# Self-attention: query and key rows of heads 4 to 15 moved into their stacks by transfers

## The chip, the cores and the metric

One core of a Trainium2 chip runs the whole program. The time is the device time of one execution in microseconds, the median of three runs for the kernel before. Its engines are TensorE (PE, with its weight loads as PEld), VectorE (DVE), ScalarE (ACT), GpSimd (POOL) and SyncE (SP), which here only issues transfers.

## The reference, cut to what matters

Four sequences of 1024 tokens with 256 channels pass through four blocks: an expert block (its own stage of the program, not touched but for one order), and then two transformer blocks and a last cross-attention. All is float32. The first transformer block:

```python
t_sa, t_ca, t_mlp = jnp.split(jax.nn.silu(t_emb) @ tp_w + tp_b, 3, axis=-1)
h = layernorm(x, ln1_g, ln1_b)
h = mha(h, h, sa_wq, sa_bq, sa_wk, sa_bk, sa_wv, sa_bv, sa_wo, sa_bo)      # 16 heads of 16
x = x + h + t_sa[:, None, :]
h = layernorm(x, ln3_g, ln3_b)
h = mha(h, context_emb, ca_wq, ca_bq, ca_wk, ca_bk, ca_wv, ca_bv, ca_wo, ca_bo, mask=mask)   # 77 context rows
x = x + h + t_ca[:, None, :]
h = layernorm(x, ln2_g, ln2_b)
x = x + jax.nn.gelu(h @ w1 + b1, approximate=False) @ w2 + b2 + t_mlp[:, None, :]
# mha: softmax(q k^T / 4) v for each head
```

The second block is the same with modulated norms (weights `L2_...`, query, key and value in one matrix `qkv_w`); the third has one cross-attention. So there are 4 x 2 = 8 self-attentions, 12 cross-attentions and 8 MLPs in a run.

## The kernel before

The program is one Bass block for each engine. The four sequences pass one after the other through the loop `blocks`. The order of the work in one pass is the list `PASS`, which `pass_schedule` writes out; every engine walks that list and does its part of each step, and semaphores count the steps. The names are tuples: a module (`L1sa`, `L1ca`, `L1mlp`, `L2sa`, ...) and a step. `n` is a half of 512 tokens, `c` a half of the 256 channels, `g` a group of four heads.

In a self-attention the steps are: `N` normalise, `T` transpose, `P` project queries or keys (128 channels, 512 tokens), `V` values, `K` stacks, `A` products for the row maxima, `both` and `M` the maxima's minima and transpose, `S` scores, `PV` products with the values, `O`, `R`, `W`, `Q`, `OT`, `aT` the outputs, `o` output projection.

A product of float32 precision is made of a high part (`qh`, `kh`, float32r) and a residual (`ql`, `kl`) that GpSimd computes (L1937). The stacks `qs` and `ks` hold for each pair of heads, one at partitions 0 to 63 and one at 64 to 127, the rows of 16 channels three times (high, high or low, low), so that one product gives all three terms. Two more rows hold the negated row maxima in `qs` (`MAXROW`) against ones in `ks`, and a mask. A `K` step fills the stacks of its pairs with selection products on TensorE (`sel`, two for each pair), and a copy on ScalarE (`a`, `A`) or VectorE (`d`) with a bias that sets the row of ones. `A`, `a` differ in whether the product reads all 128 rows or the pair's own 32.

`A` (g, n, t, j) is a pair of products into two banks of PSUM; VectorE reduces 128 x 1024 numbers to two maxima (L1791). There are 4 x 2 x 4 x 4 = 128 of them, of which 20 stand before the first scores. After that the list has for each unit of four score products (`S`, one for each head of a group, exponential on ScalarE, L1470) three further `A` steps in the first four units, and two later, until all are done. A unit is (g, n, kt), 64 in all; the first eight are group 0, half 0, and the ninth begins group 0, half 1.

SyncE issues its transfers in an order of its own (`send_outputs`, which walks the same list). After each block of 128 tokens it sends the maxima of four heads into their rows of `qs` (`send_maxima`, L655, four transfers of 512 bytes), for the very first half from the transposed `mrow` (L669). `S` of unit (g, n, 0) waits until all of that group and half have landed (`maxima_stacked`). The MLP's weights come at the start of a pass (L636, L637) and, for the second block, behind the first MLP.

TensorE takes PSUM banks in a self-attention from `shared`: before the last of the first 16 maxima any of seven, later fixed ones; bank 7 sums `PV`.

## Time and profile before

| | us |
|---|---|
| three runs | 3683.58, 3699.18, 3698.08 |
| median | 3698.08 |
| profiled execution | 3701.89 |
| its span, first to last instruction | 3700.1 |
| TensorE busy in the span | 3394.4 (92%) |
| ScalarE busy | 2302.2 (62%) |
| VectorE busy | 2223.0 (60%) |
| GpSimd busy | 871.0 (24%) |

The passes of `blocks` begin at about 641, 1407, 2171 and 2934 us. A busy TensorE is not one at its peak, and the busy share is a mean over stages with different limits. It has to be read stage by stage: how full each engine is in a stretch, and which wait ends last there. The granted clock (PEclk) is 1.00 at 2.4 GHz and 0.50 at 1.2 GHz.

### The profile page before, as it was taken

What the parts mean: (1) busy time and instruction counts of PE and PEld (TensorE: products, weight loads), DVE (VectorE), ACT (ScalarE), POOL (GpSimd) and SP (SyncE); (2) the same over time, 40 slices, a digit from 0 to 9 for tenths busy, and PEclk for the clock granted to TensorE, in tenths of its full rate; (3) what the DMA queues carried; (4) which work ended last, traced back from release to release, by engine and by line L of the source; (5) the groups of instructions that cost most, each with busy time, mean ns of one, the idle gap of its engine ahead of it and who ended that gap; (6) DMA issues with size and microseconds to landing.
All of it is one profiled execution on the core that took longest, in us unless ns stands there. A gap on an engine that the chain in (4) does not pass through costs nothing.

```text
span 3700.1 us, 60840 instructions
## 1 busy us (share of the span) xinstructions
PE 3394.4 (92%) x22433; PEld 2000.9 (54%) x22433; DVE 2223.0 (60%) x3645; ACT 2302.2 (62%) x3983; POOL 871.0 (24%) x578
## 2 busy tenths in 40 slices
PE   8999998999899898998998889989998899899988
PEld 6767766444643564446444744455446444564465
DVE  2323324794397556953794559746955488549654
ACT  2333332787578555875786457865875578658764
POOL 0322322103400431015103420052024200340061
PEclk8989989999999999999999999999999999999999
DMA  5011012110100001110010010100100101000100
GB/s 184 1 36 35 2 36 63 32 16 26 39 8 14 13 13 57 14 30 31 13 16 15 12 57 11 22 26 26 14 19 13 58 7 26 24 28 11 22 13 13
DMA packets 226988, 101.25 MB, mean 27 GB/s; under 512 B 159951, under 2 KB 210322, under 8 KB 226582
## 3 DMA queue, kind: packets, MB, share of 16 engines
q1 hardware_dynamic: 201734, 77.21, 8.4%
q10 hardware_dynamic: 24976, 20.15, 1.8%
q8 instruction: 196, 3.21, 0.4%
q14 instruction: 82, 0.67, 0.1%
HBM read 79.31 MB, written 9.96 MB: 24 GB/s over the span
## 4 chain that ended last, share of the span: by engine, by line
PE 79%; DVE 12%; ACT 5%; issue 2%; POOL 1%; DMA 0%; SPq 0%; ACTq 0%; DVEq 0%; POOLq 0%
PE ps L736 76%; DVE mxh L1791 4%; PE ps L1184 2%; DVE ctxk L1740 2%; DVE ow L1823 1%; ACT probs L1470 1%; DVE tok L1526 1%; PE ps L1045 1%; DVE small L1510 1%; DVE x L1757 1%; DVE mx L1788 1%; POOL small L1847 1%; ACT qs L1439 1%; ACT whole L1424 1%; ACT hT L1256 1%
## 5 line engine op out<-in xcount | busy, mean ns | idle before, releaser
L1470 ACT ACTIVATE probs<-ps 128x512 f32<-128x512 f32 (+1 forms) x2176 | 1220.4, 639 | 222.3 <-PE ps L736 169.7
L1791 DVE TENSOR_REDUCE mxh<-ps 128x2 f32<-128x1024 f32 x1024 | 1232.1, 1220 | 101.2 <-PE ps L736 96.3
L736 PE MATMUL ps<-probs,v 128*32 128x256 f32 (+2 forms) x8064 | 732.8, 435 | 9.7 <-ACT probs L1470 6.3
L736 PE MATMUL ps<-ks,qs 64*128 64x512 f32 x2048 | 502.4, 491 | 51.5 <-DVE mxh L1791 23.3
L736 PEld LDWEIGHTS ps<-ks,qs 64*128 64x128 f32 x2048 | 193.0, 183 | 445.8 <-issue 347.7
L736 PE MATMUL ps<-qs,ks 64*128 64x512 f32 x2048 | 425.5, 413 | 4.0 <-DVE mxh L1791 3.0
L1911 POOL TENSOR_TENSOR hT<-hT,tok 128x512 f32<-128x512 f32 (+1 forms) x32 | 40.9, 1279 | 1221.1 <-DMA tok<-weights_of_outputs 1221.1
L736 PEld LDWEIGHTS ps<-probs,v 128*32 128x32 f32 (+1 forms) x8064 | 160.0, 107 | 302.7 <-ACT probs L1470 249.1
L736 PEld LDWEIGHTS ps<-qs,ks 64*128 64x128 f32 x2048 | 244.0, 184 | 127.6 <-ACT probs L1470 105.9
L1788 DVE TENSOR_REDUCE mx<-ps 128x4 f32<-128x312 f32 x384 | 166.3, 477 | 150.9 <-PE ps L736 147.4
L736 PE MATMUL ps<-hT,slot 128*128 128x512 f32 x448 | 235.5, 659 | 21.2 <-issue 8.5
L1439 ACT ACTIVATE qs<-ps,cols 128x512 fp32r<-128x512 f32 x288 | 180.4, 688 | 106.4 <-PE ps L736 106.0
L736 PE MATMUL ps<-slot,hT 128*128 128x256 f32 x896 | 217.6, 388 | 9.3 <-ACT hT L1485 9.3
L1847 POOL TENSOR_TENSOR small<-small 128x4 f32<-128x4 f32 x66 | 67.8, 1028 | 654.9 <-DVE small L1520 654.9
L1877 POOL TENSOR_TENSOR hidl<-hid,hidh 128x512 fp32r<-128x512 f32 x96 | 125.5, 1309 | 356.6 <-ACT hid L1348 356.4
L1757 DVE TENSOR_TENSOR x<-x,ps 128x512 f32<-128x512 f32 x80 | 54.9, 686 | 238.2 <-PE ps L736 238.2
L736 PEld LDWEIGHTS ps<-slot,hT 128*128 128x128 f32 x896 | 164.1, 190 | 60.0 <-issue 29.3
L1937 POOL TENSOR_TENSOR ql<-whole,qh 128x512 fp32r<-128x512 f32 x80 | 101.9, 1274 | 280.2 <-ACT whole L1424 280.2
L1345 ACT ACTIVATE hidh<-ps,cols 128x512 fp32r<-128x512 f32 x96 | 66.2, 689 | 162.6 <-PE ps L736 162.5
L1919 POOL TENSOR_TENSOR hidl<-hid,hidh 128x512 fp32r<-128x512 f32 x128 | 161.5, 1295 | 7.1 <-ACT hid L1494 5.8
L1045 PE MATMUL ps<-ident,tok 128*128 128x128 f32 x448 | 76.9, 310 | 80.4 <-DVE tok L1526 62.4
L736 PEld LDWEIGHTS ps<-kz,qs 128*128 128x128 f32 x768 | 123.1, 213 | 46.0 <-issue 17.6
(226 smaller groups left out, 5893.9 us busy)
## 6 DMA issues: line engine op xcount, KB each, us to landing
qs<-mx SPq DMA_DIRECT2D x896, 0.5 KB, 2.0
slot<-in_L_w SPq DMA_DIRECT2D x8, 1024.0 KB, 10.0
slot<-in_L_fc_w SPq DMA_DIRECT2D x8, 1024.0 KB, 5.2
hT<-ow SPq DMA_DIRECT2D x48, 128.0 KB, 2.7
tok<-weights_of_outputs SPq DMA_DIRECT2D x192, 32.0 KB, 1.9
xin<-in_x ACTq DMA_DIRECT2D x5, 1024.0 KB, 5.9
x_after_block<-x ACTq DMA_DIRECT2D x20, 256.0 KB, 2.3
xin<-x_after_block SPq DMA_DIRECT2D x5, 1024.0 KB, 5.5
```

The source lines that it names most:

```text
L736: return pe.matmul(out, lhsT, rhs, start=start, stop=stop)
L1045: ins = pe.transpose(ps[:, b, i * P:(i + 1) * P], tok[:, t, c * P:(c + 1) * P], ident[:])
L1184: ins = pe.transpose(ps[:, a, i * P:(i + 1) * P], ow[:, o:o + P], ident[:])
L1439: ins = act.activation(qs[:, pair, n * HALF:(n + 1) * HALF], ps[:, b, :], ACT.Identity, bias=qs_rows)
L1470: ins = act.activation(dst, src, ACT.Exp, scale=SCALE)
L1757: dve.tensor_tensor(xx, xx, src, ALU.add).then_inc(dve_done, M.add(dve_done, (tag, "x", t2)))
L1788: dve.tensor_reduce(mx[:, z, t, j0:j0 + GH], ps[:, a, 0:GH * SP_].rearrange("p (j s) -> p j s", s=SP_), AX.X, ALU.max, negate=True).then_i ...
L1791: dve.tensor_reduce(mxh[:, z, t, j // 2, j % 2, :], ps[:, a:a + 2, :], AX.X, ALU.max, negate=True).then_inc(dve_done, M.add(dve_done, name))
L1847: pool.tensor_tensor(rstd[:, tt], ve[:, tt], nhalf[:, tt], ALU.pow).then_inc(pool_done, M.add(pool_done, (tag, "rstd", h)))
L1877: pool.tensor_tensor(hidl0[:, (E * n + e) % 2, m % 4, :], hid0[:, m % 4, :], hidh0[:, (E * n + e) % 2, m % 4, :].bitcast(F32), ALU.subtrac ...
L1919: pool.tensor_tensor(hidl[:, n, m, :], hid[:, n, m, :], hidh[:, n, m, :].bitcast(F32), ALU.subtract).then_inc(pool_done, M.add(pool_done, ...
L1937: pool.tensor_tensor(lo[:, c, part], whole[:, whole_of(name)[0], 0:kn], hi[:, c, part].bitcast(F32), ALU.subtract).then_inc(pool_done, M.a ...
```

## The change

Selection products remain for heads 0 to 3 only (pairs 0 and 1 of channels 0 to 127). The rows of heads 4 to 15 are moved into their places in `qs` and `ks` by transfers from the projections' high and low parts. For this the columns of the query and key weights and biases are laid out on the host so that the heads of a group of rows lie a fixed step apart (`heads_apart`), and every second row of such a tile belongs to the same half of the pairs. Each transfer writes 16 partitions: `X` step part 1 moves two pairs (heads 4 to 7, 128 KB a transfer, into `group_moved`), part 2 four pairs (heads 8 to 15, 256 KB a transfer, into `heads_moved`). A part has twelve of these and two of ones into the maxima's row of `ks`. The stack's places are set anew (48 rows, then the maxima's and the mask's row), and the products read 48 or 49 rows instead of 64.

The projections' parts get places of their own: those of channels 0 to 127 in the exponentials' buffers 2 and 3, so the third unit's exponentials wait for part 1, and those of channels 128 to 255 in the MLP's weight slots 2 and 3. So the MLP's weights are now loaded behind part 2 of `X` in the same module, and SyncE waits there for `heads_moved`.

The lead-in has another order: 16 first maxima by key halves, projections of the other halves between them. TensorE may use all eight banks before the first scores. `A` waits for its own pair and half only. In a cross-attention `OT` stands behind the next products; in an MLP two `up` steps stand ahead of the second half's transposes, the second `rsqrt` is at its normalisation, and the split of the normalised rows goes channel half by channel half.

```diff
@@ -48,9 +48,11 @@
 FF = 4 * D
 FM = FF // P
 STACK = 64
-MAXROW = 32
-MASKROW = 33
+MAXROW = 48
+MASKROW = 49
+PLACES = {"q": ((0, 16), (32,)), "k": ((0, 32), (16,))}
 PAIRS = HEADS // 2
+PROBS_KEPT = 2
...
     def self_lead(tag):
 
         first = tag == "L1sa"
-        put(tag, ("T", 0), *[("load",)] * first, ("P", "q", 0, 0), ("P", "k", 0, 0), ("N", 1), ("T", 1), ("P", "q", 1, 0),
-            ("K", "dddd", "q", 0, 0), ("K", "aaaa", "k", 0, 0), ("P", "k", 0, 1), ("P", "q", 0, 1), ("V", 0), ("K", "ddaa", "k", 0, 1), *[("mask",)] * first)
+        put(tag, ("T", 0), *[("load",)] * first, ("P", "q", 0, 0), ("P", "k", 0, 0), ("N", 1), ("T", 1),
+            ("K", "dd--", "q", 0, 0), ("K", "aa--", "k", 0, 0), *[("mask",)] * first)
...
     def self_attention(tag, follow):
         maxima, last = [], []
+        moves = [("X", 2, which, e) for e in range(2) for which in "qk"]
         for g in range(GROUPS):
             for n in range(NH):
+                if (g, n) == (0, 0):
+                    maxima += [("A", g, n, t, j) for i in range(2) for t in range(TPH) for j in (i, 2 + i)]
+                    maxima += [("both", g, n, TPH - 1)]
+                    last = [("M", g, n)]
+                    continue
                 for t in range(TPH):
                     maxima += [("A", g, n, t, 0)] + last + [("A", g, n, t, j) for j in range(1, GH)]
-                    last = [("both", g, n, t)] if (g, n) != (0, 0) else []
-                if (g, n) == (0, 0):
-                    maxima += [("both", g, n, TPH - 1)]
-                    last = [("M", g, n)]
+                    last = [("both", g, n, t)]
+                    if g < 2:
+                        last += moves[:2]
+                        moves = moves[2:]
         maxima += last
 
-        def halves(which, c, n, who="a"):
-            return [("K", 2 * who + "--", which, c, n), ("K", "--" + 2 * who, which, c, n)]
-
-        beside = ([("P", "k", 1, 0)] + halves("q", 0, 1) + [("P", "q", 1, 1)] + halves("k", 1, 0) + [("P", "k", 1, 1)]
-                  + [w for k in halves("q", 1, 0, "A") + halves("q", 1, 1, "A") for w in (k, None)] + halves("k", 1, 1, "A"))
+        def pair_of(which, n):
+            return ("K", "aa--", which, 0, n)
+
+        beside = {2: [("P", "k", 0, 1)], 4: [("P", "q", 0, 1)], 6: [pair_of("k", 1)], 8: [pair_of("q", 1)],
+                  9: [("X", 1, which, e) for e in range(2) for which in "qk"] + [("V", 0)], 11: [("P", "q", 1, 0)], 13: [("P", "k", 1, 0)],
+                  15: [("P", "q", 1, 1)], 17: [("P", "k", 1, 1), ("add",)]}
...
-        first_slot = GH * TPH
-        for i in range(first_slot):
-            more(i + 1)
-            put(tag, *[w for w in beside[i:i + 1] if w])
-        more(first_slot + 1)
-        put(tag, *beside[first_slot:], ("add",))
-        lead = first_slot + 4
-        more(lead)
+        lead = GH * TPH + 4
+        for i in range(1, lead + 1):
+            more(i)
+            put(tag, *beside.get(i, []))
...
@@ -252,12 +257,12 @@
         for u in range(len(units) + lag):
             if u < len(units):
                 put(tag, ("S",) + units[u] + (0,), *last[4 * u:4 * u + 2])
-            if u > lag:
-                put(tag, ("OT",) + units[u - lag - 1][:2])
             if u >= lag:
                 put(tag, ("PV",) + units[u - lag], ("O",) + units[u - lag][:2])
             if u < len(units):
                 put(tag, ("S",) + units[u] + (2,), *last[4 * u + 2:4 * u + 4])
+            if u > lag:
+                put(tag, ("OT",) + units[u - lag - 1][:2])
...
-        put(follow, ("T", 0), ("N", 1), ("T", 1), *[("up", 0, m) for m in range(FM)])
+        put(follow, ("T", 0), ("N", 1), ("up", 0, 0), ("up", 0, 1), ("T", 1), *[("up", 0, m) for m in range(2, FM)])
...
-def stacks_for(tag, engine, g, n):
-
+def stacks_for(tag, engine, g, n, j):
+
+    cross = KIND[tag] == "cross"
+    pairs, halves = ((2 * g, 2 * g + 1), (0,)) if cross else ((2 * g + j // 2,), (j % 2,))
     return [(tag,) + stack for k in PASS if k[:2] == (tag, "K") for _, pair, stack, by in stack_pairs(*k[2:])
-            if by == engine and pair * 2 // GH == g and (k[3] == "k" or k[5] == n)]
+            if by == engine and pair in pairs and (k[5] in halves if k[3] == "k" else k[5] == n)]
...
+def heads_apart(a, blocks):
+
+    import numpy as np
+
+    columns = np.arange(a.shape[-1])
+    for block in range(blocks):
+        for first, heads in ((P // 2, GH), (P, 2 * GH)):
+            at = block * D + first
+            columns[at:at + heads * HD] = at + np.arange(heads * HD).reshape(heads, HD).T.ravel()
+    return a[..., columns]
...
+        kept = {(which, 0): [place(f"{which}0{part}", [P, N], F32R, offset=r2 + 4 * (PROBS_KEPT * GH * HALF + (2 * i + k) * N))
+                             for k, part in enumerate("hl")] for i, which in enumerate("qk")}
...
+        kept.update({(which, 1): [place(f"{which}1{part}", [P, N], F32R, offset=at[0] + 4 * (2 * 2048 + (2 * i + k) * N))
+                                  for k, part in enumerate("hl")] for i, which in enumerate("qk")})
...
+        def heads_of(tag, which, part, e):
+
+            c, first = (0, P // 2) if part == 1 else (1, 0)
+            dst, pairs = (qs, ks)[which == "k"], slice(PAIRS // KC // 2, PAIRS // KC) if part == 1 else slice(PAIRS // KC, PAIRS)
+            return [(dst[stacked(e, row, row + HD), pairs, :].bitcast(F32), tile[first + e:P:2, :].bitcast(F32))
+                    for tile, rows_at in zip(parts_of(tag, which, c), PLACES[which]) for row in rows_at]
...
-                sp.dma_start(W1, wide(T["L1_w1"])).then_inc(slot_loaded[2], M.add(slot_loaded[2], "L1mlp", LOADED))
-                sp.dma_start(W2, wide(T["L1_w2"])).then_inc(slot_loaded[3], M.add(slot_loaded[3], "L1mlp", LOADED))
...
+                def send_heads(tag, part, which, e):
+
+                    moved, c = group_moved if part == 1 else heads_moved, part - 1
+                    end = (tag, part) if (which, e) == ("k", 1) else None
+                    for n in range(NH):
+                        sp.wait_ge(pool_done, upto(pool_done, (tag, "P", which, c, n)))
+                    if which == "k":
+                        pairs = slice(PAIRS // KC // 2, PAIRS // KC) if part == 1 else slice(PAIRS // KC, PAIRS)
+                        sp.dma_start(ks[stacked(e, MAXROW, MAXROW + 1), pairs, :].bitcast(F32), ones[0:(pairs.stop - pairs.start) * N // 32, :]
+                                     ).then_inc(moved, M.add(moved, None, LOADED))
+                    for i, (dst, src) in enumerate(heads_of(tag, which, part, e)):
+                        sp.dma_start(dst, src).then_inc(moved, M.add(moved, end if i == 2 else None, LOADED))
+                    if part == 2 and end:
+                        sp.wait_ge(heads_moved, upto(heads_moved, end))
+                        for dst, s, name in (W1, 2, {"L1sa": "L1_w1", "L2sa": "L2_fc1_w"}[tag]), (W2, 3, {"L1sa": "L1_w2", "L2sa": "L2_fc2_w"}[tag]):
+                            then = tag[:2] + "mlp"
+                            sp.dma_start(dst, wide(T[name])).then_inc(slot_loaded[s], M.add(slot_loaded[s], then, LOADED))
...
-                    for _, kind, g, n, *rest in [k for k in PASS if k[0] == tag and k[1] in ("both", "M", "O", "R", "W")]:
+                    for _, kind, g, n, *rest in [k for k in PASS if k[0] == tag and k[1] in ("both", "M", "O", "R", "W", "X")]:
+                        if kind == "X":
+                            send_heads(tag, g, n, *rest)
+                            continue
...
-                sp.wait_ge(mm_done, upto(mm_done, ("L1mlp", "up", NH - 1, FM - 1)))
-                sp.dma_start(W1, wide(T["L2_fc1_w"])).then_inc(slot_loaded[2], M.add(slot_loaded[2], "L2mlp", LOADED))
-                sp.wait_ge(mm_done, upto(mm_done, ("L1mlp", "o", 3)))
-                sp.dma_start(W2, wide(T["L2_fc2_w"])).then_inc(slot_loaded[3], M.add(slot_loaded[3], "L2mlp", LOADED))
...
-            USED = [0] * 7
+            USED = [0] * 8
...
+                        if kind == "S":
+                            scored.add(tag)
+                        if tag in scored and asked[tag] < GROUPS * NH * TPH * GH:
                             among = (0, 2) if count == 2 else (4, 5, 6)
+                        elif tag in scored:
+                            among = range(8 - count)
                         else:
-                            count = 2 if kind == "A" else 1
-                            among = range(8 - count)
+                            among = range(9 - count)
...
-                        pe.wait_ge(act_done, upto(act_done, *stacks_for(tag, "act", g, n), *act_was))
-                        pe.wait_ge(dve_done, upto(dve_done, *stacks_for(tag, "dve", g, n), *dve_was))
+                        pe.wait_ge(act_done, upto(act_done, *stacks_for(tag, "act", g, n, j), *act_was))
+                        pe.wait_ge(dve_done, upto(dve_done, *stacks_for(tag, "dve", g, n, j), *dve_was))
...
+                            if g == 1:
+                                pe.wait_ge(group_moved, upto(group_moved, (tag, 1)))
+                            elif g > 1:
+                                pe.wait_ge(heads_moved, upto(heads_moved, (tag, 2)))
                             pair, i = 2 * g + j // 2, j % 2
                             for e in range(2):
-                                r = stacked(e, 0, STACK)
+                                r = stacked(e, 0, MAXROW)
...
                 for c in range(KC):
                     act.wait_ge(mm_done, upto(mm_done, (tag, "T", n, c)))
                     act.activation(hTh[:, c, half], ps[:, M.where((tag, "T", n, c)), :], ACT.Identity, bias=shift(c), scale=gain(c))
-                for c in range(KC):
+                    act.wait_ge(mm_done, upto(mm_done, (tag, "T", n, KC - 1)))
...
+                        if not cross and (u, j) == (PROBS_KEPT, 0):
+                            act.wait_ge(group_moved, upto(group_moved, (tag, 1)))
...
-                    elif kind == "o" and step[1] % 2 and tag in NEXT_LN:
+                    elif kind == "o" and step[1] % 2 and tag in NEXT_LN and not (step[1] == 3 and NEXT_LN[tag] in ("ln2", "ln6")):
                         rsqrt(upto, NEXT_LN[tag], step[1] // 2)
+                    elif kind == "N" and step[1] and KIND[tag] == "mlp":
+                        rsqrt(upto, ln, 1)
...
+    for n, which in (("L1_sa_wq", 1), ("L1_sa_wk", 1), ("L2_qkv_w", 2)):
+        arrays[n] = heads_apart(arrays[n], which)
```

On SyncE, in the first self-attention, behind the transfers of the first maxima. `mx` are maxima of 128 tokens, `mrow` those of the first half, `slot` the MLP's weights, `q1h` to `k1l` the parts of channels 128 to 255. Before:

```order
L636 DMA slot_102<-in_L_w 128x2x1024
L637 DMA slot_103<-in_L_w 128x8x256
L669 DMA qs<-mrow 1x4x128 x4
L655 DMA qs<-mx 1x128x1 x24
L678 DMA sums<-ow 32x1x16 x4
```

And now:

```order
L725 DMA qs<-mrow 1x4x128 x4
L690 DMA qs<-mx 1x128x1 x4
L705 DMA qs<-q1h 16x4x1024 x2
L705 DMA qs<-q1l 16x4x1024
L702 DMA ks<-ones 1x128x32
L705 DMA ks<-k1h 16x4x1024 x2
L705 DMA ks<-k1l 16x4x1024
L690 DMA qs<-mx 1x128x1 x4
L705 DMA qs<-q1h 16x4x1024 x2
L705 DMA qs<-q1l 16x4x1024
L702 DMA ks<-ones 1x128x32
L705 DMA ks<-k1h 16x4x1024 x2
L705 DMA ks<-k1l 16x4x1024
L710 DMA slot_110<-in_L_w 128x2x1024
L710 DMA slot_111<-in_L_w 128x8x256
L690 DMA qs<-mx 1x128x1 x16
```

The 24 maxima transfers in a row are now 4, 4 and 16, with seven transfers of heads behind each of the first two fours, and the wait for `heads_moved` and both weight loads ahead of the third and fourth block of the second half.

On TensorE, from the transposes of the first self-attention to the first maxima products (`ks<-qs`, two to a step `A`); `hT` with a slot are projections, rows with `sel` are selection products. Before:

```order
L1045 MATMUL ps<-ident,tok 128x128 x8
L736 MATMUL ps<-hT,slot_100 128x512 x2
L736 MATMUL ps<-qh,sel 128x512 x4
L736 MATMUL ps<-ql,sel 128x512 x4
L736 MATMUL ps<-kh,sel 128x512 x4
L736 MATMUL ps<-kl,sel 128x512 x4
L736 MATMUL ps<-hT,slot_100 128x512 x4
L736 MATMUL ps<-slot_100,hT 128x256 x4
L736 MATMUL ps<-kh,sel 128x512 x4
L736 MATMUL ps<-kl,sel 128x512 x4
L736 MATMUL ps<-ks,qs 128x512 x2
```

And now:

```order
L1100 MATMUL ps<-ident,tok 128x128 x8
L788 MATMUL ps<-q0h,sel 128x512 x2
L788 MATMUL ps<-q0l,sel 128x512 x2
L788 MATMUL ps<-k0h,sel 128x512 x2
L788 MATMUL ps<-k0l,sel 128x512 x2
L788 MATMUL ps<-ks,qs 128x512 x4
L788 MATMUL ps<-hT,slot_108 128x512 x2
L788 MATMUL ps<-ks,qs 128x512 x4
```

Three projections, the values and sixteen selection products no longer stand between the second transposes and the first maxima.

On TensorE, at the start of an MLP (`hTh`, `hTl` are the normalised rows in two parts, `W1h`, `W1l` the weights; three rows and three more are one `up` step). Before:

```order
L736 MATMUL ps<-slot_101,hT 128x256 x8
L1045 MATMUL ps<-ident,tok 128x128 x16
L736 MATMUL ps<-hTh,W1h 128x512
```

And now:

```order
L788 MATMUL ps<-slot_109,hT 128x256 x8
L1100 MATMUL ps<-ident,tok 128x128 x8
L788 MATMUL ps<-hTh,W1h 128x512
L788 MATMUL ps<-hTl,W1h 128x512
```

The second half's eight transposes stand twelve products later.

## Rows read from the trace of the kernel before

**Rows 1.** Stretches of the first self-attention: length, busy us (count) of each engine, clock, DMA.

```profile
641.00:666.70 25.70, 18.38 (x71) 9.64 (x71) 10.70 (x37) 13.42 (x21) 8.64 (x7) 0.79 0.53 168
...
697.40:722.20 24.80, 22.22 (x186) 10.99 (x186) 22.58 (x25) 17.30 (x33) 0.00 (x0) 1.00 0.06 1
722.20:832.80 110.60, 110.16 (x1055) 46.10 (x1055) 107.70 (x116) 97.83 (x182) 3.84 (x3) 1.00 0.12 16
```

**Rows 2.** The page's costliest groups: busy us, mean ns | idle before, releaser.

```profile
L1791 DVE TENSOR_REDUCE mxh<-ps 128x2 f32<-128x1024 f32 x1024 | 1232.1, 1220 | 101.2 <-PE ps L736 96.3
```

**Rows 3.** Timeline of the first lead-in: start us, us, engine, line [idle before <-releaser].

```profile
655.10 1.28 POOL L1937 TENSOR_TENSOR kl<-whole,kh 128x512 fp32r<-128x512 f32 x1 [0.44 <-ACT whole L1424]
...
656.24 0.50 PE L736 MATMUL ps<-qh,sel 32*128 32x512 f32 x4
...
658.44 2.42 ACT L1447 ACTIVATE ks<-ps,cols 128x512 fp32r<-128x512 f32 x4 [0.82 <-PE ps L736]
658.57 3.67 PE L736 MATMUL ps<-hT,slot 128*128 128x512 f32 x8
...
662.07 1.89 PE L736 MATMUL ps<-slot,hT 128*128 128x256 f32 x8
...
666.75 1.23 DVE L1791 TENSOR_REDUCE mxh<-ps 128x2 f32<-128x1024 f32 x1 [0.51 <-PE ps L736]
```

**Rows 4.** Timeline, SyncE's maxima transfers, and TensorE's first scores of half 1.

```profile
704.64 2.40 SPq L655 DMA_DIRECT2D qs<-mx  x4
...
714.88 2.85 SPq L655 DMA_DIRECT2D qs<-mx  x4
...
721.79 0.40 PE L736 MATMUL ps<-qs,ks 64*128 64x512 f32 x2
```

**Rows 5.** Transfers of the first pass: count, KB each, median us from issue to landing.

```profile
qs<-mx SPq DMA_DIRECT2D x224, 0.5 KB, 2.0
...
slot<-in_L_fc_w SPq DMA_DIRECT2D x2, 1024.0 KB, 5.3
hT<-ow SPq DMA_DIRECT2D x12, 128.0 KB, 2.7
tok<-weights_of_outputs SPq DMA_DIRECT2D x48, 32.0 KB, 1.9
...
sums<-ow SPq DMA_DIRECT2D x48, 2.0 KB, 1.7
```

**Rows 6.** Timeline from the 16th maxima reduction to the second half's first transfers.

```profile
688.44 1.21 DVE L1791 TENSOR_REDUCE mxh<-ps 128x2 f32<-128x1024 f32 x1
...
690.62 2.56 SPq L669 DMA_DIRECT2D qs<-mrow  x4
...
694.78 1.09 ACT L1470 ACTIVATE probs<-ps 128x512 f32<-128x512 f32 x2 [1.09 <-PE ps L736]
...
697.45 1.23 DVE L1791 TENSOR_REDUCE mxh<-ps 128x2 f32<-128x1024 f32 x1 [2.17 <-PE ps L736]
...
698.78 0.54 SPq L655 DMA_DIRECT2D qs<-mx  x1
```

**Rows 7.** Timeline of the first cross-attention: two maxima transfers of 16 KB, and their waiter.

```profile
905.49 1.30 SPq L645 DMA_DIRECT2D qs<-mrow  x2
...
908.38 0.14 PEld L736 LDWEIGHTS ps<-qs,kz 64*77 64x77 f32 x2 [0.20 <-DMA qs<-mrow]
```

**Rows 8.** Stretches at the first MLP's start, columns as in rows 1.

```profile
936.70:939.90 3.20, 0.00 (x1) 0.00 (x0) 2.00 (x9) 2.12 (x3) 2.48 (x3) 0.76 0.88 322
940.00:945.00 5.00, 4.27 (x13) 3.25 (x14) 1.72 (x3) 2.63 (x4) 1.26 (x2) 0.50 0.01 3
```

**Rows 9.** Timeline at the first MLP's start: residuals on GpSimd, first product.

```profile
938.39 2.54 POOL L1854 TENSOR_TENSOR hTl<-whole,hTh 128x512 fp32r<-128x512 f32 x2
...
942.76 0.78 PE L736 MATMUL ps<-hTh,W1h 128*128 128x512 f32 x1
```

**Rows 10.** What TensorE's turning of the outputs (L1184) waited for, whole run.

```profile
  DVE ow L1823: 31.7, 72
```

32 lines of the change are left out of this document (19 added, 13 removed).

## The prediction

> **What bounds the kernel now.** I read the stretches of the first self-attention first. In its steady stretch TensorE is busy 110.16 of 110.60 us and VectorE 107.70, at full clock: the two are level, with ScalarE at 97.83 [rows 1]. The bound is the maxima: 1024 reductions of 1220 ns in the run, 128 for each of the eight self-attentions [rows 2], so 156 us of the 220 us that a self-attention takes can't be shortened on VectorE. Nothing given back ahead of that stretch is lost later, and nothing lost there is made good: the steady stretch has no slack. So I look at two points. The first is when the first reduction starts: 666.75, behind a lead-in of 25.7 us in which VectorE is busy 10.70 [rows 1, 3]. The second is the pacing of the stretch from 697.4 to 722.2: VectorE is busy 22.58 of 24.80 [rows 1], and at 721.79 TensorE begins the scores of the second half (group 0, half 1) [rows 4]. These scores wait for all sixteen maxima transfers of that half. Their last four are issued at 714.88 over 2.85 us and land some 2.0 us later, near 719.6 [rows 4, 5]. So that wait has 2 us to spare today. All times below are those of the first self-attention; the other seven have the same program.
>
> **The lead-in, a gain of 10 us.** Before, TensorE has to do the projections of key half 1 and query half 1 (3.67 us), the value projection (1.89 us) and all stacks of channels 0 to 127 before the first reduction [rows 3]. Now the first reduction needs the transposes, two projections and the stacks of two pairs. What ends last is GpSimd's key residual, done at 655.10 + 1.28 = 656.4. The selection products of key stacks (0.5 us where four pairs took 1.1), one copy on ScalarE (2.42 us for four) and one product bring VectorE's first reduction to about 658.2 [rows 3]: 8.5 us earlier. From there to the end of the 16th reduction it was 666.75 to 689.65, 22.9 us [rows 3, 6]. Now a projection (1.9 us) and two maxima products (0.86) stand on TensorE for every 2.44 us of VectorE, a few tenths over; with five projections, one value projection and two stack steps I get 20.6 us. That is 2.3 us more. The rest of the chain is as before: transpose, copy, four transfers from 690.62, first exponential 694.78, 21st reduction 697.45 [rows 6]. Some tenths are lost where projections now stand between these, so I take 10 us. Without anything else, the scores of the second half would begin at 711.8 instead of 721.8. The 48 selection products and 24 copies that go away for each self-attention are not a term of their own: they lay in the lead-in and beside the first 16 reductions, and this is what they give.
>
> **The first transfers (heads 4 to 7), nothing.** Twelve of 128 KB and two of ones, issued as soon as GpSimd has both halves' residuals, near 666. At 0.64 us an issue [rows 4] they take SyncE 9 us, to 675; even at 105 GB/s (below) their 1.57 MB are in by 682. The four maxima transfers queued behind them are wanted at 680.6, so they are covered. The cover is thin: at a third less speed they would delay the first scores.
>
> **The second transfers (heads 8 to 15), the loss.** On SyncE they stand between the maxima transfers of the second half, and behind the last of them SyncE waits until all have landed, then issues the two MLP weight loads, and only then the last eight maxima transfers of that half. Those queued behind the waiting instruction are exactly the ones for which TensorE waits before the second half's scores; the maxima products behind these scores on TensorE wait too, and so does VectorE. The first maxima transfers of the half go out at 698.78 - 10 = 688.8 [rows 6] and take 4 x 0.64 us, to 691.3. Seven transfers, 4.5 us, to 695.8; four maxima, to 698.3; seven transfers, to 702.8. Their last landing is either some 2 us behind the last issue, 705, or 691.3 + 1.7 + D, where D is the time in which 12 x 256 KB = 3.15 MB can be written into 16 partitions at a time. 1.7 us is what a transfer of 2 KB takes [rows 5].
>
> D is not in the trace, so I bound it by the nearest rows. 1 MB into 128 partitions lands 5.3 us after issue, 3.6 over the small one: 290 GB/s. 128 KB into 64 partitions takes 2.7, 1.0 over it: 131 GB/s [rows 5]. 16 KB into a single partition: the last of two issues ends at 906.79, so it began near 906.14, and TensorE's load that waits for it goes at 908.38, 2.2 us later; 2 KB into one partition took from 692.6 to 694.2, 1.65 us. The 0.58 us between them is 28 GB/s [rows 6, 7]. So the rate falls with the partitions written. For 16 of them the transfers of the output weights, 32 KB each, are issued every 0.42 us without a delay that shows (1.9 us) [rows 5]: at least 78 GB/s. At most it is the 131 of 64 partitions. I take the middle, 105 GB/s, D = 30 us; the bounds are 24 and 40 us.
>
> Then all is landed at 691.3 + 1.7 + 30 = 723. The two weight loads are issued (1.5 us), then eight maxima transfers (5 us), to 729.5, and landed at 731.5. The loads' 2 MB lie ahead of them in the same queue: 5.3 us for the first, 3.6 more for the second [rows 5], 732. So the scores of the second half begin at 732 instead of 721.8: **10.2 us later** than before, although 10 us had been won. TensorE stands for some 20 us meanwhile. After a pause of 3.2 us in the MLP's start its granted clock is 0.50 for the next 5 us [rows 8]; in a stretch where TensorE has no slack this costs half of that, 2.5 us. Together +12.7 us for each self-attention, +102 us for eight.
>
> In one sentence apart: the Trainium skill, SBUF — State Buffer, section "Door 1: The DMA port swizzle", says that partitions 0 to 15 reach 4 of the 16 ports, and gives 104 GB/s for a 1 MiB write to them; by this D would be 30.2 us and the sum the same, while by the 290 GB/s of the 128-partition row the transfers would end with their issue, which is the first rival. The one-partition row agrees with the 27.6 GB/s that this section has for one port.
>
> **MLP start, a gain of 16 us.** TensorE has finished the first half's transposes at 936.7 [rows 8] and starts the first product at 942.76, because the second half's transposes stand before it; GpSimd has the first half's residuals at 938.39 + 2.54 = 940.9 [rows 9]. Now two products' groups stand ahead of the second transposes, and start at 940.9 or a little earlier: 1.9 us, eight MLPs, 15 to 16 us. The reciprocal root that moves behind these residuals on GpSimd delays only the second half's normalisation, which the two groups (2.8 us) and the rest of the first half cover.
>
> **Cross-attention, a gain of 10 us.** Turning the outputs waits 31.7 us in the run for VectorE's copy [rows 10]. Moved behind the next products it finds the copy done. Where ScalarE or VectorE is the bound the time is only moved, so I count a third: 10 us, between 0 and 30. The other orders (split of the normalised rows, an eighth bank in the lead-in, 48 or 49 rows instead of 64 in the products) I put at nothing: the products stream 512 columns either way.
>
> **Sum.** 102 - 16 - 10 = +76 us. The profiled execution took 3701.9 us (span 3700.1), 3.8 over the median of 3698.1; I add to the median: **3774 us**. With D = 24: 8 x (10.2 - 6 + 2.5) - 26 = +28, 3726. With D = 40, and the first transfers then 3 us late: 8 x (20.2 + 2.5 + 3) - 26 = +180, 3878.
>
> **Rivals.**
> 1. The transfers keep up with their issue (faster). If writes to different groups of partitions overlap, all is landed at 705. Weight loads at 706.5, last maxima issued at 711.5 and landed at 713.5, or at 714 behind the loads: the scores start 2.2 us behind 711.8, 7.8 earlier than before, with no pause worth a clock. 8 x -7.8 - 26 = -88: **3610 us**. For it: the row of 16 partitions shows no delay at 78 GB/s, so it gives no ceiling. Against: the one-partition and the 64-partition rows, both far below the 290.
> 2. Half of that (no change): an effective 150 to 160 GB/s, as when the tail of one transfer overlaps with the next. D = 20: 8 x (0.2 + 2.5) - 26 = -4: **3694 us**. The turning point lies here: above 155 GB/s the change pays, below it costs.
> 3. Sixteen partitions get only half of what 64 get, 65 GB/s. D = 48, and the first transfers take 24 us from 667, which delays the first scores by 7: 8 x (28.2 + 2.5 + 7) - 26 = +276: **3974 us**. Against: the weights' transfers would run late at 0.42 us an issue.
>
> **How the numbers follow.** Forecast (D from 24 to 40) 0.63, first rival 0.16, second 0.11, third 0.10. The predicted time is that of the forecast. The range takes in the forecast's bounds and the second rival, and leaves out the first and the third: 3665 to 3880, 0.8 with the tails between. 0.5% (18 us) is about what a measurement of this kernel can tell: faster 0.20, same 0.09, slower 0.71; the forecast's own lower end, 3726, is slower.
>
> **What would show it.** Right: first reduction about 17 us after the first transposes instead of 21; a wait of TensorE for the maxima transfers of about 20 us, once in each self-attention, at the ninth unit of scores, with SyncE waiting for the moved heads just before; a half clock behind it; a steady stretch as long as before. Wrong if the last of the second transfers lands within 12 us of the first one's issue, or if the first exponential comes no earlier (then the lead-in's 10 us were not there), or if the steady stretch changes its pace of 1.24 us a maximum.

## The result, and the profile after

The changed kernel takes **3906.3 us** (median of 5 runs, 3873.8 to 3921.9) where the kernel before takes 3698.1: ratio 1.057, 95% interval 1.054 to 1.060. That is 208 us more; I had forecast 76 more, and 3880 as the upper end. The profiled execution is the shortest of the five: 3873.75 us, span 3872.0, mean clock 0.915 (before: 3700.1 and 0.963). The four others had clocks of 0.905 to 0.912. That execution therefore spent about 2 x (1 - 0.915) x 3872 = 658 us at the lower of TensorE's two clocks (1.2 GHz), where before it was 274. Of the runs below, one execution of orders (5198 us at a clock of 0.549) and one of heads_behind (4559 us at 0.638) are far from all others of their kernel and are left out of medians and ratios.

The page of the changed kernel: first the chain of waits with its shares by engine and by line, then three of its costliest groups (busy us, mean ns | idle before, releaser), then DMA issues (count, KB each, median us to landing).

```profile
PE 74%; DVE 8%; ACT 5%; DMA 5%; SPq 3%; POOL 2%; issue 2%; ACTq 0%; DVEq 0%
PE ps L788 71%; DMA ks<-k1l 3%; DVE mxh L1853 2%; DVE ctxk L1802 2%; SPq L690 1%; PE ps L1243 1%; ACT probs L1531 1%; DMA qs<-mx 1%; ACT qs L1498 1%; PE ps L1100 1%; DVE x L1819 1%; POOL hidl L1983 1%; SPq L705 1%; DVE small L1571 1%; POOL hTl L1916 1%
...
L1853 DVE TENSOR_REDUCE mxh<-ps 128x2 f32<-128x1024 f32 x1024 | 1231.9, 1220 | 387.6 <-PE ps L788 382.8
L788 PE MATMUL ps<-qs,ks 49*128 49x512 f32 x2048 | 452.4, 435 | 157.8 <-DMA qs<-mx 136.7
...
qs<-q1h SPq DMA_DIRECT2D x32, 256.0 KB, 8.6
ks<-k1h SPq DMA_DIRECT2D x32, 256.0 KB, 13.2
slot<-in_L_w SPq DMA_DIRECT2D x8, 1024.0 KB, 7.1
```

The maxima cost what they did, 1024 of 1220 ns [rows 2], but VectorE is now idle 387.6 us in front of them instead of 101.2. TensorE's scores wait 136.7 us for the maxima's transfers, and a moved head (ks<-k1l) and SyncE stand in the chain, where before the chain had 0% of either. Over eight self-attentions 136.7 us are 17 each, and they come at one place. The first of them, in stretches (PE, PEld, DVE, ACT, POOL busy; granted clock; DMA share; GB/s):

```profile
645.00:677.60 32.60, 27.07 (x80) 11.53 (x80) 24.07 (x21) 12.34 (x21) 8.57 (x7) 0.84 0.37 50
677.60:710.00 32.40, 29.53 (x191) 15.56 (x191) 22.57 (x25) 19.08 (x35) 3.49 (x1) 0.85 0.71 78
710.00:729.50 19.50, 0.19 (x3) 0.04 (x1) 1.41 (x2) 0.13 (x1) 0.00 (x0) 0.53 0.70 143
729.50:743.00 13.50, 13.50 (x82) 4.58 (x82) 6.57 (x8) 7.23 (x14) 0.00 (x0) 0.54 0.07 12
...
755.00:835.00 80.00, 79.50 (x768) 33.70 (x767) 77.99 (x84) 70.59 (x133) 2.89 (x3) 1.00 0.13 16
```

The steady stretch, last line, is that of before [rows 1]: TensorE busy 79.50 of 80, full clock. Ahead of it stand three things that before did not have: a clock of 0.84 and 0.85 in the lead-in, 19.5 us in which the engines all but stand still, and 13.5 us in which TensorE is busy throughout at half clock (0.54). Before, the clock was 1.00 from 697.4 on [rows 1] and already in the stretch ahead of that:

```profile
666.70:697.40 30.70, 27.39 (x108) 13.47 (x107) 23.62 (x21) 19.33 (x32) 8.37 (x4) 1.00 0.01 1
```

The chain of waits there, start, duration, what:

```profile
699.01 18.99 DMA ks<-k1l
...
718.02 0.39 SPq L710
...
718.45 0.47 SPq L710
...
718.97 0.59 SPq L690
...
723.62 5.80 DMA qs<-mx
...
729.46 5.75 PE ps L788 x26
```

The last moved head is issued at 699.01 and lands 18.99 us later. Then come the two weight loads, the maxima's transfers, and 5.80 us from the issue of the last that is needed to its landing, behind 2 MB of weights. Where a self-attention's time goes, as the mean of the eight in each profiled execution (read from the timelines: first transposes, first exponential, 9th, 17th and 33rd unit, last exponential), with the median of the kernel's executions:

| kernel | transposes to 1st exp. | to unit 9 | to 17 | to 33 | to the end | all | outside of the eight | median |
|---|---|---|---|---|---|---|---|---|
| before | 48.5 | 27.5 | 20.1 | 40.2 | 77.7 | 214.0 | 1988 | 3698 |
| changed | 44.3 | 52.2 | 27.1 | 40.2 | 77.7 | 241.6 | 1939 | 3906 |
| orders | 48.8 | 27.6 | 20.1 | 40.2 | 77.7 | 214.4 | 1956 | 3673 |
| orders_warm | 47.1 | 27.8 | 20.1 | 40.2 | 77.7 | 213.1 | 1956 | 3663 |
| wait_behind | 44.6 | 45.0 | 28.4 | 40.8 | 77.7 | 236.5 | 1958 | 3851 |
| heads_behind | 44.5 | 33.5 | 27.9 | 44.6 | 77.7 | 228.2 | 1959 | 3786 |
| filled | 43.9 | 54.5 | 20.7 | 40.2 | 77.7 | 237.0 | 1954 | 3861 |
| spread | 44.6 | 33.1 | 25.5 | 44.9 | 77.8 | 225.9 | 1956 | 3771 |
| spread_filled | 45.6 | 27.6 | 26.0 | 45.4 | 77.7 | 222.4 | 1960 | 3726 |
| apart | 45.5 | 48.3 | 30.3 | 40.2 | 77.7 | 242.0 | 1953 | 3874 |
| apart_spread | 45.8 | 27.7 | 21.0 | 40.8 | 77.8 | 213.2 | 1948 | 3661 |
| apart_all | 44.2 | 28.0 | 21.2 | 41.7 | 77.8 | 212.9 | 1945 | 3659 |

For the changed kernel: 8 x 27.6 = +221 inside, -49 outside, +172 for this execution. The other 36 us of the 208 are not in its profile: it was the shortest of the five.

### The profile page after: what moved, and what is told of

Same layout as the page of the kernel before. It is cut to its first block, busy times and chain, and to the rows that moved or that the text cites. A ratio compares the mean times of both kernels' runs of the same rounds, so it can differ in the third digit from the quotient of the medians.

```text
span 3872.0 us, 59985 instructions
## 1 busy us (share of the span) xinstructions
PE 3426.2 (88%) x22049; PEld 1989.7 (51%) x22049; DVE 2197.2 (57%) x3614; ACT 2202.8 (57%) x3823; POOL 871.4 (23%) x578
## 4 chain that ended last, share of the span: by engine, by line
PE 74%; DVE 8%; ACT 5%; DMA 5%; SPq 3%; POOL 2%; issue 2%; ACTq 0%; DVEq 0%
PE ps L788 71%; DMA ks<-k1l 3%; DVE mxh L1853 2%; DVE ctxk L1802 2%; SPq L690 1%; PE ps L1243 1%; ACT probs L1531 1%; DMA qs<-mx 1%; ACT qs L1498 1%; PE ps L1100 1%; DVE x L1819 1%; POOL hidl L1983 1%; SPq L705 1%; DVE small L1571 1%; POOL hTl L1916 1%
## 5 line engine op out<-in xcount | busy, mean ns | idle before, releaser
L1853 DVE TENSOR_REDUCE mxh<-ps 128x2 f32<-128x1024 f32 x1024 | 1231.9, 1220 | 387.6 <-PE ps L788 382.8
L788 PE MATMUL ps<-probs,v 128*32 128x256 f32 (+2 forms) x8064 | 764.4, 452 | 11.2 <-ACT probs L1531 6.3
L788 PE MATMUL ps<-qs,ks 49*128 49x512 f32 x2048 | 452.4, 435 | 157.8 <-DMA qs<-mx 136.7
L788 PE MATMUL ps<-ks,qs 48*128 48x512 f32 x2048 | 513.2, 510 | 43.7 <-DVE mxh L1853 18.4
L788 PEld LDWEIGHTS ps<-ks,qs 48*128 48x128 f32 x2048 | 200.3, 195 | 465.0 <-issue 351.6
L788 PEld LDWEIGHTS ps<-qs,ks 49*128 49x128 f32 x2048 | 255.2, 195 | 293.9 <-DMA qs<-mx 139.6
L788 PE MATMUL ps<-slot,hT 128*128 128x256 f32 x896 | 259.8, 443 | 9.3 <-ACT hT L1546 9.3
L788 PEld LDWEIGHTS ps<-slot,hT 128*128 128x128 f32 x896 | 189.0, 220 | 61.8 <-issue 21.2
L1498 ACT ACTIVATE qs<-ps,cols 128x512 fp32r<-128x512 f32 x208 | 130.3, 687 | 85.0 <-PE ps L788 85.0
L788 PEld LDWEIGHTS ps<-hT,slot 128*128 128x128 f32 x448 | 88.0, 214 | 122.6 <-issue 101.1
L788 PE MATMUL ps<-W2h,hidh 128*128 128x256 f32 x512 | 145.8, 285 | 0.0
L788 PE MATMUL ps<-W2h,hidl 128*128 128x256 f32 x512 | 145.6, 284 | 0.0
```

The lines of the kernel that those rows point to most:

```text
L788: return pe.matmul(out, lhsT, rhs, start=start, stop=stop)
L1498: ins = act.activation(qs[:, pair, n * HALF:(n + 1) * HALF], ps[:, b, :], ACT.Identity, bias=qs_rows)
L1853: dve.tensor_reduce(mxh[:, z, t, j // 2, j % 2, :], ps[:, a:a + 2, :], AX.X, ALU.max, negate=True).then_inc(dve_done, M.add(dve_done, name))
```

## Experiments: the parts that were to gain, alone

**orders** is the kernel before with the three orders only.

```diff
+            if u > lag:                                    # behind the next products
+                put(tag, ("OT",) + units[u - lag - 1][:2])
...
+        put(follow, ("T", 0), ("N", 1), ("up", 0, 0), ("up", 0, 1), ("T", 1), ...)
...
+                    act.wait_ge(mm_done, upto(mm_done, (tag, "T", n, KC - 1)))     # in place of `for c in range(KC):`, one loop for both copies
...
```

Not shown is that the MLP's second `rsqrt` stands at its normalisation.

> The kernel before, with three edits of the change alone: the order of the copies of the split normalised rows on ScalarE, the two first product groups of the MLP ahead of the second transposes (with its reciprocal root behind), and the turning of the cross-attention's outputs behind the next products. Stacks, transfers and the lead-in are those of before. My prediction had 16 us for the MLP's start, 10 for the cross-attention and nothing for the copies: about 3672 us. The profile of the changed kernel says more: outside the eight self-attentions (from a self-attention's first transposes to its last exponential) it took 49 us less than before, 15 of them ahead of the first self-attention, where only the order of the copies differs. If these 49 us come from the orders: 3649 us. If the 15 us ahead of the first self-attention are only TensorE's clock falling out differently from run to run, that stretch is as long as before (645 us to the first transposes) and the time is near 3664.

Measured: 3673.4 us, ratio 0.994 (0.992 to 0.996), 22 us less than before by that ratio. The first transposes come at 644.0, as before (645.4), and in the seven other runs with the new order of the copies and nothing added ahead of them at 636.0 to 644.4. So the 15 us ahead of the first self-attention in the changed kernel's profile belong to that execution, not to the change: the clock there was 0.94 where it was 0.92 before, and the profile of rates, whose code there is that of the kernel before, has 0.94 too and came to this point at 631.5. My 26 us for the MLP's start and the cross-attention were nearly right in sum. Their two parts can't be told apart here: from the end of a self-attention to the MLP's first product the eight stretches are 41 us shorter together, and behind that product they are 10 us longer. In the changed kernel the residual now ends last, and the product follows it at once (timeline, idle in brackets; before it was 1.8 us behind [rows 9]):

```profile
945.72 2.60 POOL L1916 TENSOR_TENSOR hTl<-whole,hTh 128x512 fp32r<-128x512 f32 x2 [5.16 <-ACT whole L1325]
...
948.46 0.77 PE L788 MATMUL ps<-hTh,W1h 128*128 128x512 f32 x1 [3.64 <-POOL hTl L1916]
```

The wait for VectorE's copy in front of the turning fell from 31.7 us in 72 places [rows 10] to 6.6 in 12; the list of what that line waited for begins so in orders:

```profile
  issue: 22.1, 36
  ACT probs L1470: 10.3, 40
  ACT hT L1485: 10.1, 12
  DVE ow L1823: 6.6, 12
```

## Experiments: the stall

**wait_behind**: SyncE's wait and the weight loads behind the last maxima of group 1.

```diff
-                    if part == 2 and end:
-                        sp.wait_ge(heads_moved, upto(heads_moved, end))
-                        ... W1, W2
+                            if (g, n, rest[0]) == (1, 1, TPH - 1):
+                                load_weights(tag)          # the same wait and the two loads
```

> The changed kernel, with SyncE's wait for the moved heads 8 to 15 and the two weight loads behind it put behind the last maxima transfers of group 1 (half 1). The transfers themselves stay between the maxima transfers of group 0, half 1. Theory A, the wait is what blocks the maxima: the last eight maxima transfers go out at once, but lie behind the moved heads in the same queue, whose last one lands 30 us after the first one's issue; they land some 2 us behind it, near 720 where they landed near 729, so the scores of the second half begin 9 to 10 us earlier in each self-attention: 8 x 9.5 = 76 us less than the changed kernel, near 3830. Rival B, small transfers pass the large ones in the queue: the scores begin at 705 to 710 instead of 730, and with no pause of TensorE the clock stays up, over 200 us less, near 3680. Rival C, nothing moves since TensorE is blocked by something else: within 10 us of the changed kernel.

3850.9 us, 55 less than changed; the stretch to unit 9 takes 45.0 instead of 52.2. That is theory A, with 7 of the 9.5 us: nothing stands in SyncE's way any more, the last maxima transfers go out from 709.29 on, and TensorE still waits 9.25 us in the first self-attention.

```profile
730.00 0.86 PE L792 MATMUL ps<-qs,ks 49*128 49x512 f32 x2 [9.25 <-DMA qs<-mx]
```

The four maxima transfers that are issued last there, from 717.20 on, land 11.2 to 12.0 us after their issue, behind the last moved head, which lands at 728.57. So small transfers do not pass large ones issued before them on this queue. The Trainium skill says why that is to be expected, in DMA: Bandwidth & Descriptors, section "Queues, rings and completion order": a transfer's completion is a write that lands only after every earlier write of that DMA engine. The next run agrees: there, in the second self-attention, the 0.5 KB of maxima behind six moved heads land 5.6 to 12.8 us after issue, where 2.0 is the median before [rows 5].

**heads_behind**: the moved heads, six at a time, also behind the maxima that are due first.

```diff
-                    if g < 2:
+                    if (g, n, t) in ((0, 1, TPH - 1), (1, 0, TPH - 1)):
                         last += moves[:2]
```

> As the one before (wait and weight loads behind group 1's last maxima), and the transfers of heads 8 to 15 also moved: six behind the last maxima transfer of group 0, half 1, six behind that of group 1, half 0. So no maxima transfer of group 0 stands behind a moved head. Theory A (the transfers' time of 2.2 us for each 256 KB, in front of the maxima, is the whole stall): the pause of 19 us at the ninth unit is gone, TensorE's clock does not fall there, and the 97 us from the first exponential to the unit 32 shrink from 118 to about 88, as before the change. That takes off some 27 us for each self-attention; with 49 us from outside the self-attentions the time is then 3698 - 49 - 8 x 3 = 3625. Rival B: the stall only moves, since the maxima of group 1, half 0, or the products of group 2 then wait for the same 27 us of transfers: a wait of 5 to 15 us at unit 16 or at the 65th maximum, 3700 to 3780.

3786.5 us: rival B, a little above its range. The pause of 19 us is gone, and the wait has moved to something that I had not counted, the sums of the outputs, on VectorE. Timeline, then stretches, second self-attention:

```profile
1092.43 0.25 DVE L1884 RECIPROCAL sums<-sums 128x16 f32<-128x16 f32 x1 [3.63 <-DMA sums<-ow]
1092.60 1.16 DVE L1857 TENSOR_REDUCE mxh<-ps 128x2 f32<-128x1024 f32 x1
...
1093.86 0.50 PE L792 MATMUL ps<-ks,qs 48*128 48x512 f32 x2 [3.06 <-issue]
```

```profile
1077.50:1094.00 16.50, 13.32 (x132) 5.58 (x131) 12.42 (x15) 12.33 (x23) 0.00 (x0) 1.00 0.95 73
1094.00:1105.00 11.00, 11.00 (x68) 3.91 (x72) 7.61 (x8) 5.66 (x11) 0.00 (x0) 0.57 0.76 95
```

VectorE waits 3.63 us for 2 KB that lie behind moved heads. TensorE stands for 3.06 us; the profile names no releaser, but its product starts 0.10 us behind the end of VectorE's next reduction, so I read it as waiting for that. Then it works 11 us without a gap at 0.57. In the first self-attention the same happens behind a wait of 3.55 us, and there TensorE works 37.5 us without a gap at 0.50. A wait in the steady stretch is paid twice.

**spread**: two of the moved heads behind each of six steps, with SyncE's wait and the weight loads where wait_behind has them.

```diff
+        moves = [("X", 2, which, e, i) for e in range(2) for which in "qk" for i in range(3)]
+                    if (g, n, t) >= (0, 1, TPH - 1):
                         last += moves[:2]
...
```

> The changed kernel, with the twelve transfers of heads 8 to 15 issued two at a time behind the maxima of each of the six steps from the last of group 0, half 1 on, and the wait for them with the two weight loads behind group 1's last maxima. In the run where they went six at a time, the small transfers of the sums lay 14 us behind them, VectorE waited 3.6 us for these, TensorE 3.1 us for VectorE, and its clock then stood at 0.50 for 10 us. Theory A (what costs is only that small transfers lie in the queue behind large ones of 2.2 us each, and the clock behind the pause): with two at a time no small one is late by more than 5 us, no wait of TensorE over 1.5 us is left behind the 21st maximum, and units 9 to 32 take 60.3 us as before the change instead of 68 to 79. Then each self-attention ends where it did before, plus 1 to 5 us that the lead-in's half clock costs: 3672 + 8 x 3, near 3696, and over 80 us under the kernel with six at a time. Rival B (2.2 us for each transfer is still too much, since the maxima and sums have less than 4 us to spare): a wait of 2 to 5 us at one of the units 9 to 32, near 3750.

3771.4 us: again B, and worse than it said. Two waits are left in the first self-attention, 1.87 and 1.54 us, and behind the second TensorE is busy for 26.3 us on end at 0.55, which is half clock for some 24 of them:

```profile
735.91 0.25 DVE L1886 RECIPROCAL sums<-sums 128x16 f32<-128x16 f32 x1 [2.46 <-DMA sums<-ow]
737.34 0.50 PE L794 MATMUL ps<-ks,qs 48*128 48x512 f32 x2 [1.87 <-issue]
...
745.63 0.57 PE L794 MATMUL ps<-qs,ks 49*128 49x512 f32 x2 [1.54 <-DMA qs<-mx]
```

```profile
746.20:772.50 26.30, 26.30 (x161) 8.79 (x164) 15.17 (x17) 14.63 (x27) 0.00 (x0) 0.55 0.35 51
```

## Experiments: the clock

**filled**: the changed kernel, and products in front of the wait of group 0, half 1, where `b` is the bank of the scores that follow and `at` the first column of the other half.

```diff
+                for i in range(80):
+                    mm(ps[:, b, :], qs[:, 0, at:at + P], ks[:, 0, :])
                 pe.wait_ge(maxima_stacked[g][n], upto(maxima_stacked[g][n], (tag, 1)))
```

> The changed kernel, with 80 products of 128 rows by 512 columns, whose result is overwritten, in front of TensorE's wait for the maxima of group 0, half 1; everything else as changed. They fill the pause of 19.3 us (80 at 0.23 us is 18.4 us), so TensorE works through it, and nothing starts earlier. Theory A (the pause costs twice, once for itself and once for the half clock behind it, 4 to 14 us between the 9th and the 17th unit): the granted clock stays at 1.00 behind the pause, units 9 to 16 take 20 us as before instead of 24 to 34, and the kernel takes 8 x 4 to 8 x 14, about 60 us less than the changed kernel, and its runs lie closer together. Rival B (the slow units behind the pause have another cause, such as the transfers or the late vector work): same time as the changed kernel, or 0 to 8 x 1 us more.

3861.0 us, ratio 1.044 (1.042 to 1.046), 45 less than changed, with four executions within 17 us where the five of changed lie within 48. Units 9 to 16 take 20.7 us on average instead of 27.1; seven of eight take 20.1 or 20.2, and in the eighth, where 3.2 us of wait were left over, they take 24.2. The stretch to unit 9 grew by some 2 us, since the products overran the wait (54.5 for 52.2). That is theory A:

```profile
722.00:739.50 17.50, 17.50 (x82) 14.06 (x84) 0.00 (x0) 0.03 (x1) 0.00 (x0) 1.00 0.56 138
739.50:759.60 20.10, 19.97 (x196) 8.41 (x196) 18.60 (x21) 17.73 (x33) 0.00 (x0) 1.00 0.11 16
```

Without them, in the changed kernel's last self-attention, TensorE stood until 3518 and then needed 34 us, busy in every one of them, for the same 196 products:

```profile
3518.00:3552.00 34.00, 34.00 (x196) 11.06 (x200) 18.91 (x21) 17.86 (x33) 0.00 (x0) 0.51 0.07 10
```

**spread_filled**: spread, with eight such products in the wait for the first 16 maxima and eight in front of the first scores.

> As the one before, with eight products of 128 rows by 512 columns, whose result is overwritten, in TensorE's wait for the first 16 maxima (2.2 us), and eight in its wait for the maxima's transfer in front of the first scores (2.1 us). Theory A (the lead-in loses what its earlier start gained to the clock: after these two waits it stands at 0.50 for 12 us, so the stretch from the first exponential to the ninth unit takes 33.8 us instead of 27.4): with the waits filled that stretch is 27 to 29 us, some 5 us less for each self-attention, 40 us less than the kernel without them, near 3655. Rival B (the stretch is longer because projections and value products were moved into it): it stays at 33 to 34 us, and the time is the same within 8 us.

3726.1 us, 45 less than spread; I had said 40 less (my 3655 stood on a spread of 3696). The stretch from the first exponential to unit 9, spread above and spread_filled below:

```profile
688.30:722.20 33.90, 30.94 (x197) 16.18 (x201) 23.17 (x26) 19.35 (x35) 3.66 (x1) 0.80 0.15 17
```

```profile
691.30:718.70 27.40, 24.84 (x196) 12.86 (x200) 22.62 (x25) 18.98 (x35) 1.68 (x1) 1.00 0.19 20
```

The same products, 6.5 us less, and the clock 1.00 instead of 0.80. So what this stretch had lost, it had lost to the clock, not to the work moved into it (rival B).

**orders_warm**: orders, with filled waits in the experts, at a pass's start and at the MLP's start.

> The kernel before with the three orders of the change (3672 us), and with products of 128 rows by 512 columns, whose result is overwritten, in TensorE's longest waits: 18 in the 4.2 us between two batches of the experts (three times), 60 and then 20 in front of a pass's first transposes (14.3 us in the first pass, 5.0 in the others), 15 in the 3.6 us in front of an MLP's first product (eight times). Theory A (a wait of TensorE costs a second time, by the half clock behind it): half clocks of 10 us behind the waits of the experts, 17 and 10 in a pass's start and 3 to 7 in an MLP's start go away, which is worth half of them where TensorE is the bound: 15 + 12 + 16 = some 40 us, near 3630. Rival B (the clock falls for what TensorE does next, products of few rows, and not for the wait): the stretches at half clock stay, within 8 us of 3672 or slower by the products' overrun.

3662.6 us, ratio 0.992 (0.990 to 0.995). The mean clock went from 0.964 to 0.978 but the time only 11 us down instead of 40. The experts came 21 us earlier (first transposes at 623.4), the self-attentions gained 11 in sum, and the stretches between them lost 20: 32 from the end of a self-attention to the MLP's first product, against 12 gained behind it. The 15 products in front of an MLP explain a part: in seven of the eight they ran at a mean clock of 0.68 to 0.72 and took 5.0 to 5.3 us in a wait of 3.6, 11 us in the run. Where the other 21 went is open; none of the three sets was tried alone.

## Experiments: the rate

**rates**: the kernel before, and six sets of four transfers behind its end (the time has nothing to say).

```diff
+                    tests = ([t[0:16, 2 * i:2 * i + 2, :] for i in range(4)],
+                             [t[32 * i:32 * i + 16, 0:2, :] for i in range(4)],
+                             [t[0:P:8, 2 * i:2 * i + 2, :] for i in range(4)],
+                             [t[0:32, i, :] for i in range(4)],
+                             [t[0:64, i, 0:HALF] for i in range(4)],
+                             [t[0:P, i, 0:HALF // 2] for i in range(4)])
```

> The kernel before, and behind its last product six sets of four transfers from SBUF to SBUF, 128 KB each, each from 32 partitions of 4 KB, and each set waited for: into partitions 0 to 15 (8 KB each); into 16 partitions in four groups that begin at 0, 32, 64 and 96, one after the other; into every eighth of the 128 partitions; into 32 partitions; into 64; into 128. Theory A (the partitions written set the rate, by where they lie): 1.1 us for one transfer in the first two sets (117 GB/s, as the moved heads had), about half of that or less where the 16 are spread over all 128, and the less the more partitions are written. Rival B (the rate is set by the reading side, 32 partitions, or by the length of a row of 4 KB, alike in all sets): 1.1 us in the sets into 16 and 32 partitions wherever they lie. Rival C (the number of partitions alone counts): the spread 16 as slow as the first 16. [...]

Us from issue to landing in the first three sets, in the order of the code:

```profile
DMA to landing us min/median/max: 3.1/4.6/5.0
...
DMA to landing us min/median/max: 3.3/4.2/4.7
...
DMA to landing us min/median/max: 2.5/2.6/2.6
```

In the first two each transfer lands later behind its issue than the one ahead: the four land over 3.9 and 3.2 us, on average 1.29 and 1.07 us apart, 102 and 122 GB/s (the first set followed the last stores of the outputs, and its gaps shrink from 1.84 to 0.82 us, so its 102 is the less certain). In the third, 16 partitions as well but eight apart, they follow the issue of 0.64 us, at least 205 GB/s. 32 neighbouring partitions: 0.76 us apart, 172 GB/s; 64 and 128: as issued. So theory A; B and C fall. The Trainium skill, SBUF — State Buffer, section "Door 1: The DMA port swizzle", gives the port of each partition: by its table partitions 0 to 15 lie on 4 of the 16 ports, four to a port, and sixteen partitions eight apart lie on 8 ports, two to a port. The trace agrees in kind, with 102 and at least 205 GB/s. Sixteen partitions three apart, which the next run uses, also reach 8 ports by that table, but three of them share the fullest one; with the section's 27.6 GB/s for one port my estimate is 27.6 x 16 / 3 = 147 GB/s, and the next run shows some 142.

**apart**: the changed kernel with interleaved rows.

```diff
-PLACES = {"q": ((0, 16), (32,)), "k": ((0, 32), (16,))}
+PLACES = {"q": ((0, 1), (2,)), "k": ((0, 2), (1,))}
-                            out[..., STACK * e + row + d] = 1.0
+                            out[..., STACK * e + row + 3 * d] = 1.0
-            dst[stacked(e, row, row + HD), pairs, :]
+            dst[STACK * e + row:STACK * e + 3 * HD:3, pairs, :]
```

> The changed kernel with one thing changed: the 48 rows of a head's stack are interleaved. High, low and high parts of dimension d stand in rows 3d, 3d+1, 3d+2, where each part had 16 rows together; so each transfer of moved heads writes 16 partitions spread over 48. Bytes, order of issue, waits and products are the same. In the set of transfers measured alone, 128 KB took 1.29 us into partitions 0 to 15, 1.07 us into four groups in turn, 0.76 us into 32 neighbouring ones, and no more than the 0.64 us of an issue where the 16 were spread over all 128. Theory A (the place of the partitions sets the rate, and this rate was the right term of my sum): a transfer of 256 KB takes 1.3 to 1.6 us instead of 2.2, the twelve are in 16 to 19 us instead of 28, and the scores of the second half begin some 10 us earlier in each self-attention, with less half clock behind: 80 to 110 us under the changed kernel, 3800 to 3825. Rival B (for rows this close the rate stays at 117 GB/s): no change, 3890 to 3920.

3873.6 us (3848 to 3906; the longest is left out of the ratio, and without it the median is 3856), ratio 1.048 (1.041 to 1.055): 33 less than changed, where A said 80 to 110 and B none. The four executions overlap those of changed and the two intervals touch, so the size of this gain is not well known. The rate rose less than I had thought: some 1.85 us for 256 KB, 142 GB/s, and 25.8 us from the first issue to the last landing instead of 30.4. TensorE's wait in the first self-attention is 13.49 us instead of 19.31,

```profile
738.77 0.86 PE L788 MATMUL ps<-qs,ks 49*128 49x512 f32 x2 [13.49 <-DMA qs<-mx]
```

and units 9 to 16 behind it take 30.3 us on average instead of 27.1, most of that at half clock: TensorE works 17 to 34 us on end at 0.50 there, 11 to 34 in changed. The shorter wait was given back there and in the lead-in, in this execution entirely (242.0 for 241.6). Why the clock stayed down longer behind a shorter wait is open.

**apart_spread**: interleaved, spread, and with the two filled waits of the lead-in; it differs from spread_filled in the rows alone.

> The interleaved rows together with the transfers two at a time and the products in the two waits of the lead-in (that kernel took 3726 us with 16 rows together). There TensorE still waited 2.1 us in the steady stretch, behind VectorE's wait for sums that lay in the queue behind two moved heads (4.4 us), and stood at half clock for 3 to 44 us after it. Theory A (each small transfer lies behind the large ones' time, so faster ones remove the wait): with 2.6 to 3.2 us for two of them the wait and the half clock behind it go in most self-attentions, the stretch from the 9th to the 33rd unit takes 60.3 to 62 us instead of 62 to 82, and the time is 3726 - 8 x 7 = near 3670. Rival B (the wait comes from SyncE's issue of 0.6 us for each of 14 more transfers, which faster data doesn't shorten): the wait stays, 3715 to 3735.

3661.4 us, ratio **0.992 (0.989 to 0.994)**: theory A. The same edit of the rows that was worth 33 us in the changed kernel is worth 65 here, since the waits it shortens are those behind which the clock fell: units 9 to 16 need 21.0 us instead of 26.0, and 17 to 32 need 40.8 instead of 45.4. First self-attention:

```profile
683.40:710.80 27.40, 24.84 (x197) 12.81 (x200) 22.59 (x25) 19.01 (x35) 1.69 (x1) 1.00 0.15 21
710.80:732.00 21.20, 20.13 (x198) 8.57 (x200) 19.23 (x22) 17.76 (x33) 0.00 (x0) 1.00 0.59 102
732.00:772.80 40.80, 40.09 (x388) 17.06 (x391) 38.80 (x43) 35.53 (x67) 0.29 (x1) 1.00 0.41 87
```

**apart_all**: with the filled waits of orders_warm as well (and 7 instead of 8 products in each wait of the lead-in).

> As the one before, and with the products in TensorE's waits between the experts' batches, in front of a pass's first transposes and in front of the MLP's first product that took the three orders alone from 3676 to 3663 us. Theory A: these add up, 10 to 20 us less than the kernel before it: 3650 to 3660 where that one takes 3670. Rival B (the steady stretches lose at half clock what the rest gains): within 5 us of it.

3659.5 us, 0.992 (0.990 to 0.994): within 5 us of the one before, rival B in size; its steady stretches did lose a little (41.7 for 40.8). So the kernel before is beaten by three versions that can't be told apart, 3659 to 3663 us. Two of them move the heads and one does not, and the interval of orders alone, at 3673, overlaps theirs. The transfers of the heads, with all that was wrong about them mended, are worth at most some 12 us (8 by the ratios), of which the filled waits may be a part. The new lead-in without transfers was not run.

## Why the prediction was wrong

**What bounds the kernel, right.** The steady stretch is untouched in every run (77.7 us behind unit 33, and 1.24 us a maximum), so all that happens ahead of it reaches the end undiminished.

**Which steps failed.** Two terms of the sum, the gain of the lead-in and the half clock behind the stall. heads_behind has no stall ahead of unit 9, and there the two stretches up to that unit take 44.5 + 33.5 = 78.0 us where before they took 76.0. So the lead-in's -10 us was +2. The +2.5 us of half clock behind the stall was +7.0. The stall itself, 732 - 711.8 = 20.2 us in my sum, measured 52.2 - 33.5 = 18.7. Together 12.0 + 4.5 - 1.5 = 15.0, and a self-attention grew by 27.6 where I had 12.7.

**The lead-in, a gain of 10 us: wrong, in the chain behind its first link.** The first reduction came 6.9 us earlier in the first self-attention and 8.0 on average (I had said 8.5, and named the key residual and the two pairs' stacks rightly). From there on the gain melts: start of the 17th reduction 5.9 earlier, first exponential 4.2, and in the first self-attention the 21st reduction 1.1 later than before. Timeline of the changed kernel, its first transposes at 630.55:

```profile
641.66 1.27 POOL L2001 TENSOR_TENSOR k0l<-whole,k0h 128x512 fp32r<-128x512 f32 x1 [1.60 <-ACT whole L1483]
...
645.03 1.23 DVE L1853 TENSOR_REDUCE mxh<-ps 128x2 f32<-128x1024 f32 x1 [1.59 <-PE ps L788]
...
670.21 0.30 PE L1190 MATMUL ps<-ident,mx 128*16 128x128 f32 x1 [2.17 <-DVE mx L1865]
670.33 3.64 PE L788 MATMUL ps<-hT,slot 128*128 128x512 f32 x4
...
676.95 0.59 PE L788 MATMUL ps<-qs,ks 49*128 49x512 f32 x1 [2.08 <-DVE mxh L1853]
```

The projection in the middle is the step that I got wrong in small: 1.9 us by my count, 3.64 here, since TensorE had stood for 2.17 us and the clock was down. I had priced the moved projections at full clock because the lead-in of before ran at it. Spread_filled shows what is lost by that: 5.5 us a self-attention between the first exponential and unit 9, where that stretch is back to 27.6 for the 27.5 of before. Even so it reaches unit 9 only 2.7 us earlier than before and not 10; up to its first exponential the clock still stood at 0.85 to 0.90 and VectorE waited up to 3.2 us at a time for TensorE, behind moved projections and value products. How the missing 7 us divide between clock and projections was not tried. "Not a term of their own" was wrong of the selection products too: they had been filling TensorE's time between projections. That this is what kept the clock up is my reading; only the filling of the waits was tried.

**The first transfers, nothing: right.** In by 667.9 (I had said 682), since they went out from 652.8 and not from 666; no wait for them in any profile.

**The second transfers: the mechanism right, its place too early and its tail too short.** D was right: 30.4 us from the first issue to the last landing, I had 31.7, with 2.1 to 2.3 us for 256 KB (some 119 GB/s, I took 105). But the first of them was issued 57 us behind the first transposes and not 46: the lead-in's missing 11 us. And behind the last landing it took 11.5 us to TensorE's first scores, not 9. So the scores of the second half come 22.5 us later than before in the first self-attention and not 10.2. Of the rest, wait_behind gives SyncE's wait with the loads 7 us of the 25 that the stretch lost, and heads_behind all but 6 of what remains; those 6 are the clock, as spread_filled shows for 5.5 of them.

**+2.5 us for the clock: mis-sized nearly threefold.** I took it from one row of 5 us [rows 8] behind a pause of 3.2. Behind this pause the clock stayed down for 11 to 34 us of unbroken work, which cost 7.0 us a self-attention on average and 14 in the worst; filled took 45 us off the whole run. The four other executions took 20 to 48 us more at clocks of 0.905 to 0.912. The slowest spent, by its clock and span, some 745 us at half clock instead of 658; half of these 87 would be 43 of its 48 us. That is an estimate, and no profile shows in which stretches they lie.

**MLP and cross-attention, -26: right in sum** (orders: -22; the changed kernel's profile: -34 apart from the first stretch). The order of the split, which I had put at nothing, was not run apart from these. **48 and 49 rows, nothing: right** in the steady stretch.

Split by the table's stretches, the same 15 us are: 5.8 that the lead-in did not gain (4.2 for 10), 4.6 in the stretch to unit 9 (24.8 for 20.2, and 6 of these 24.8 are the clock that fell in the lead-in), and 4.5 of the clock behind the pause. The chances were wrong in their basis too: my range varied D, the one term that came out as told, and held the clock's and the lead-in's terms fixed.

**Rivals.** The first two needed a rate above 150 GB/s, and the trace excludes it: the last transfer lands 30 us behind the first's issue. The third came nearest in size (+276 for the measured +208, where the forecast had +76), but by a wrong cause, half the rate: that would have been luck.

## What to carry to other kernels

A wait in a stretch where TensorE has no slack is paid twice: price the half clock behind it by how long a saturated stretch has been seen to keep it, and put that into the range, not at one value. A large transfer delays every small one issued behind it on its queue, so count all small ones that come due while it runs, those of other engines' sums included. Sending the large ones in twos was not enough here while each took 2.2 us; it was once their rows lay apart. When work is taken from a lead-in that runs at full clock, ask whether it was filling TensorE's waits.

## What the runs showed of the hardware

- TensorE, busy without a gap, stayed at half clock (1.2 GHz) for some 24 us after waits of 1.87 and 1.54 us (spread), for 37.5 us after one of 3.55 us (heads_behind, first self-attention), and for 34 us after one of 18.1 us (changed kernel, last self-attention). Of the other seven in the changed kernel, behind waits of 11.6 to 20.8 us, six had the full clock back after 11 to 15 us and one after 30. In the kernel before the clock stood at 1.00 through the lead-in's waits of up to 1.6 us. What decides between these was not found. The Trainium skill, TensorE: Matmul & The Clock Gate, section "What's actually happening", puts the penalty of the ramp below 1% of a typical kernel's span; here filling one wait in each self-attention took 45 us off 3906, 1.2%, and the executions spent 4 to 19% of their time at the lower clock, so for this kernel the measurement decides against it.
- Transfers into 16 neighbouring partitions: 102 to 122 GB/s; 16 partitions three apart some 142; 32 neighbours 172; 16 partitions eight apart at least 205.
- Transfers of 0.5 KB issued behind six of 256 KB on one queue landed 5.6 to 12.8 us after their issue (heads_behind), where 2.0 is the median before.
